# The last layer's attention output on one Trainium2 core: both products turned by matmuls with the identity into one place, without VectorE's sum

## What is computed

```python
scores = jnp.einsum('biph,biqh->biqp', k, q)
tril = jnp.tril(jnp.ones((n, n), dtype=scores.dtype))
triu = jnp.triu(jnp.ones((n, n), dtype=scores.dtype))
masked = scores * tril - NEG_BIG * (1.0 - triu)
attn = jax.nn.softmax(masked / D_HEAD ** 0.5, axis=-1)
z = jnp.einsum('biph,biqp->biqh', v, attn)
z_flat = jnp.transpose(z, (0, 2, 1, 3)).reshape(b, n, -1)
out = jnp.einsum('df,bqf->bqd', W_O, z_flat)
```

## Time and profile before

| | |
|---|---|
| device time, median of 3 runs | 3890.96 us (3883.97 to 3895.62) |
| the profiled execution | 3896.18 us |
| its span | 3893.9 us |
| mean granted TensorE clock | 0.887 of full speed |
| busy: VectorE, TensorE, ScalarE, GpSimd | 88%, 80%, 75%, 34% of the span |

### The profile page before, as it was taken

One profiled execution on the slowest core, in us unless ns is written; L12 is line 12 of the kernel. 1 busy time (PEld: TensorE's weight loads), 2 busy tenths in 40 slices (PEclk: granted clock), 3 DMA queues, 4 the chain that ended last, 5 costly groups with the idle time before them and its releaser, 6 DMA issues.

```text
span 3893.9 us, 31221 instructions
## 1 busy us (share of the span) xinstructions
PE 3127.3 (80%) x8728; PEld 1368.3 (35%) x8728; DVE 3420.1 (88%) x4654; ACT 2925.3 (75%) x3806; POOL 1337.2 (34%) x644
## 2 busy tenths in 40 slices
PE   5655878889787788979888888979788887877797
PEld 3231423334343333424343333424343333432232
DVE  1499979999898999999999999999999998999822
ACT  2546887987868888787888878787888879686442
POOL 0254333333323334343433443343433433333200
PEclk8757788989888899989999999989989999888797
DMA  1233333424324243333434342343424333333310
GB/s 63 77 108 96 113 109 92 128 80 135 99 94 118 93 131 95 119 118 109 125 98 123 107 131 94 121 117 109 124 95 126 104 116 104 104 119 104 100 49 11
DMA packets 209022, 404.60 MB, mean 104 GB/s; under 512 B 25936, under 2 KB 34256, under 8 KB 208592
## 3 DMA queue, kind: packets, MB, share of 16 engines
q1 hardware_dynamic: 206800, 398.41, 32.8%
q0 software_dynamic: 2048, 4.20, 1.0%
HBM read 387.57 MB, written 14.94 MB: 103 GB/s over the span
## 4 chain that ended last, share of the span: by engine, by line
PE 37%; DVE 26%; ACT 25%; issue 12%; POOL 0%; DMA 0%; DVEq 0%; ACTq 0%; POOLq 0%
PE bank_a L569 8%; DVE states L921 7%; PE bank_b L580 7%; ACT L705 6%; DVE states L927 6%; ACT decay L705 6%; DVE y_sum L932 3%; ACT L701 3%; ACT tok L705 3%; ACT last L705 3%; ACT middle L705 3%; PE bank_p L478 1%; PE bank_c L397 1%; PE bank_p L421 1%; PE bank_c L640 1%
## 5 line engine op out<-in xcount | busy, mean ns | idle before, releaser
L1199 POOL TENSOR_TENSOR dbu<-dtu,b_rows 128x1024 f32<-128x1024 f32 x512 | 1243.4, 2431 | 2104.1 <-DVE states L921 1823.6
L921 DVE TENSOR_TENSOR_SCAN states<-decay,dbu 128x512 f32<-128x512 f32 x1024 | 1298.7, 1311 | 38.1 <-ACT decay L705 30.5
L705 ACT ACTIVATE decay<-dt,neg_a 128x508 f32<-128x508 f32 x1024 | 659.4, 707 | 64.6 <-DVE states L921 59.0
L705 ACT ACT_TABLE_LOAD x516 | 662.0, 1283 | 47.5 <-PEq L344 16.6
L569 PE MATMUL bank_a<-middle,experts 128*128 128x512 f32 x1024 | 616.2, 687 | 97.1 <-ACT middle L705 88.9
L705 ACT ACTIVATE middle<-bank_a,columns 128x512 f32<-128x512 f32 x608 | 417.8, 687 | 329.6 <-PE bank_a L569 305.4
L927 DVE TENSOR_TENSOR states<-states,c_rows 128x512 f32<-128x512 f32 x960 | 610.8, 679 | 0.3
L932 DVE TENSOR_TENSOR y_sum<-y_sum,states 128x512 f32<-128x512 f32 x960 | 609.9, 674 | 0.2
L580 PE MATMUL bank_b<-middle,experts 128*128 128x512 f32 x1024 | 572.7, 643 | 21.4 <-ACT middle L705 11.8
L705 ACT ACTIVATE last<-bank_c 128x512 f32<-128x512 f32 (+2 forms) x320 | 201.0, 634 | 198.0 <-PE bank_c L617 52.4
L701 ACT ACT_TABLE_LOAD x232 | 297.7, 1283 | 46.0 <-PE bank_p L469 17.0
(11 more groups left out here) (206 smaller groups left out, 3944.7 us busy)
## 6 DMA issues: line engine op xcount, KB each, us to landing
b_rows<-bc_scratch SPq DMA_DIRECT2D x512, 256.0 KB, 3.4
c_rows<-bc_scratch SPq DMA_DIRECT2D x512, 256.0 KB, 3.3
experts<-ew SPq DMA_DIRECT2D x128, 512.0 KB, 3.5
comb_rows<-comb_scratch SPq DMA_DIRECT2D x128, 256.0 KB, 3.8
h_scratch<-tok SPq DMA_DIRECT2D x16, 256.0 KB, 3.3
x_scratch<-xin SPq DMA_DIRECT2D x16, 256.0 KB, 3.8
xr<-x_scratch SPq DMA_DIRECT2D x16, 256.0 KB, 4.9
h<-h_scratch SPq DMA_DIRECT2D x16, 256.0 KB, 5.3
```

The source lines that it names most:

```text
L705: return nc.scalar.activation(out, in_, func, **more)
L921: tick(nc.vector.tensor_tensor_scan(hs[:, h, ::step], da[:, n % DECAYS, h, ::step], dbu[:, n % AHEAD, h, ::step], 0.0, ALU.mult, ALU.add), ...
L1199: tick(nc.gpsimd.tensor_tensor(dbu[:, n % AHEAD], dtu[:, k % 2], row, ALU.mult), "a_dbu")
```

## The change

The sum on VectorE goes, with the semaphore `a_z`. `zu` becomes two tiles in turn, as `zs` has, and the second of them is `h3`, which the layer doesn't need at that time. TensorE waits for both products and turns each 128x128 block of both by a matmul with the identity; the second adds into the place of the first. The four order strings of TensorE, ScalarE, VectorE and SyncE are written anew from early on. All pieces are still there, but for VectorE's 64 pieces with the sum; TensorE's string keeps its 2836 letters, VectorE's has 2759.

```diff
@@ ORDER (lines from each string, the rest is like it)
-        "PDCPPPPPPPPPPPPCPPPPPPPPPPPPPPPPPPPPPPPPPPPPPPPPPPPDDDPDCPDPDPPDDPDDPPDPPDPPPPPPPPPPPPPPPPPPPPPPPPPP"
+        "PDCPPPPPPPPPPPPCPPPPPPPPPPPPPPPPPPPPPPPPPPPPPPPPPPPDDPDDPCDPDPPPPPDDPPDDPPDPDPPPPPPPPPPPPPPPPPPPPPPP"
...
-    d_sq, d_xn, h3, zu = (fin[:, i] for i in (0, 1, 2, 5))
+    d_sq, d_xn, h3 = (fin[:, i] for i in (0, 1, 2))
+    zu = fin[:, 5], h3
...
                     else:
                         yield
-                        pe.wait_ge(s["a_z"], x + j + 1)
+                        pe.wait_ge(s["a_zu"], 2 * (x + j + 1))
                         for pr in range(4):
-                            last = nc.tensor.transpose(bk[:, blk(pr)], zs[j % 2][:, blk(pr)], w("ident"))
+                            mm(bk[:, blk(pr)], zs[j % 2][:, blk(pr)], w("ident"), start=True, stop=False)
+                            last = mm(bk[:, blk(pr)], zu[j % 2][:, blk(pr)], w("ident"), start=False, stop=True)
                         tick(last, "a_T")
...
                     tick(tt(eight(z), eight(v[:, j]), wide(e1[:, h]), ALU.mult), "a_zu")
                     yield
-                    if x + j:
-                        dve.wait_ge(s["a_z"], x + j)
                     dve.wait_ge(s["a_sv"], x + j + 1)
-                    tick(tt(eight(zu), eight((C, E)[j % 2]), wide(e0[:, h]), ALU.mult), "a_zu")
-                    yield
-                    dve.wait_ge(s["a_zu"], 2 * (x + j + 1))
-                    tick(tt(z, z, zu, ALU.add), "a_z")
+                    tick(tt(eight(zu[j % 2]), eight((C, E)[j % 2]), wide(e0[:, h]), ALU.mult), "a_zu")
```

More of the change, by code:

```diff
@@ new lines @@
+        "CCCPCCCPCCCPCCCCPCCPPCCPPCCPPCCPCCPPCCDCCDCCDDCCPCCDPCCDCPCCCPDCDDDPPCCDPPCCDPPCCPPDDPDPDCPDPCPDDDDD"
+        "DCDCPDDPCPDCPPDPCCCPDDCCPDCCCCPCDCPPDCCPPDDCCDPPDCCPDCCPCCPCCPCCPCCDDPDPCCPPDCCPPCCPDDDDPCCDCCPCCPDD"
+        "DPDCCDCCDDCCCCDCCDCCCCDCCDCCCCCCCCPDDCPCCPCDPPDCPPCCDPPCCDPCCPCDPCDDDPDCPPDCPDDDCDCDDDCCCPCCDPPDDCCD"
+        "PPCCPPCDCPCCPCCDPPDCCDPPDCCPPDCCPDCCPCCPCDCCCPDPDPCCPPDCCPPCCDPPCCDPDCCPDPDDDCCDCCDCCDCCDDCCPCCDCCDC"
+        "CCCCCCCPCCPCDCCPDCDDPPCDPCCPDPPCCPPPDDPCCPCDPCPDCDDCDDPDCDDCPPDPPDDCCCPPDCCPDPCCDPPDDPPCCDPCCPCCDPDC"
@@ new lines @@
+        "CDCCPCCPCCDCCPDCCPCCDPDCCPPDCCPPCCDPPCCPDCCPCCPCCDDDPDDCCCCPCCDCCDCDCPCCDDCCCCDDCCCCPDCCPDPCPCCPPCPP"
+        "DDCPPDDCCDCCDCCPCPCPPDDDCCDDDDDCDDPDCPPDPPDDCCCPPDCCPDCCDCCDCCDPPPDCCPPDCCPPDDCCPDDCCPCCPCCPCCPCCDPC"
+        "CDPPCCDPPCCPPDPDCCDCCPDDPDDPCCCCDCCDCCDCCDDCCDDCCCCDCCDCCCCCCDCCPCPDCCPDDCPPCDPPCCDPPCCPPPDDCCCPCPDP"
+        "CPDCDDDDCDDDCDDCCCPCCDPPCCDPPDPPDDCCPDCCDCCPCCDPPDCCDPPDCCDPCCPCCDPDCCPCCPCCPCCDPDPCCPPCCPDCCPPPCCPD"
+        "DCCPDPDDPCCCCDCCDCCDCCDCCDCCDDCCCPCDPCCDPPPCCPPCDCCDCPPCDDPCCPCCDPCCDPPPDPDDDDDDCDPCDDPPDCPPCDPPDDPC"
@@ new lines @@
+        "DCPDCCPCPDDCCDPPCCDCCPCPDCCCPDDCCPCCPCCPCCPDDPDCCPPCCDPPCCDPPCCPPPDDPCCDCCDCDDCCCDDCCCCDCCDCCDDCCDDC"
+        "CDCCDCCCCCCCCPCCPCCDDPDDPCPPCCPCPPDPDPCPDDCCPCCPCCDCPPCDDDDCDCDDPDCPPDCPPDDCCCPPDCCPDPCCDPPDDPPCCDCC"
+        "PCCPCCDPDDPDCCPCCPCCPCCDDPCCPPDCCPDPCCPPDPDCCPCCPCDCDDPDDCCCCCCCCDCCDDCCDCCDCCDDCCCCDPCCDCCPCCPCCPPC"
+        "DCCPPCDCDDPPCCPDPCCPDPPPPDDDCCCDPCDDPPDCPPCDDPCPDDCPDDDCCCPCCDPPDCCDPDDPCCPPDCCPDPCCPCCDCCPCCPCCDDDP"
+        "CCDCCPCCPPDPCCDPPCCDDPCCPCPDCCCDDDDPCCCCCCCCDCCDDDDCCDDCCCCDCCDCCCCCCPCCPCDDCCPDDCPPCDPPCCDPPCCPPPDD"
@@ new lines @@
+        "CCPCPDCPPDDCDCDDPDCDDCPPDPPDDCCCPPDCCPDCCDCCDCDCPPPDCCPPDCCPPDDCCPDDCCPCCPCCDCCPDPDPCCPPCCDPPCCDPPCC"
+        "PDDCCPDPDDPCCCCCCDCCDDDDCCDDCCCCDCCDCCCCPCCCPCCCDDPDCCPPCDPCCPCPPDPDCPPPCCCCPCCDDCPDCPDDCDDDCDDPDCPP"
+        "DCPPDDCCCPPDCCPDPCCDPPDDPPCCDCCPCCPCCDPDDPDCCPCCPCCPCCDDPCCPPDCCPDPCCPPDPDCCPCCPCDCDDPDDCCCCCCCCDCCD"
+        "DCCDCCDCCDDCCCCDPCCDCCPCCPCCPPCDCCPPCDCDDPPCCPDPCCPDPPPPDDDCCCDPCDDPPDCPPCDDPCPDDCPDDDCCCPCCDPPDCCDP"
+        "DDPCCPPDCCPDPCCPCCDCCPCCPCCDDDPCCDCCPCCPPDPCCDPPCCDDPCCPCPDCCCDDDDPCCCCCCCCDCCDDDDCCDDCCCCDCCDCCCCCC"
@@ new lines @@
+        "PCCPCDDCCPDDCPPCDPPCCDPPCCPPPDDCCPCPDCPPDDCDCDDPDCDDCPPDPPDDCCCPPDCCPDCCDCCDCDCPPPDCCPPDCCPPDDCCPDDC"
+        "CPCCPCCDCCPDPDPCCPPCCDPPCCDPPCCPDDCCPDPDDPCCCCCCDCCDDDDCCDDCCCCDCCDCCCCPCCCPCCCDDPDCCPPCDPCCPCPPDPDC"
+        "PPPCCCCPCCDDCPDCPDDCDDDCDDPDCPPDCPPDDCCCPPDCCPDPCCDPPDDPPCCDCCPCCPCCDPDDPDCCPCCPCCPCCDDPCCPPDCCPDPCC"
+        "PPDPDCCPCCPCDCDDDDCCCCCCDCDCCCDCCDCCDCCDDCCCCDCCDCCCCCCCDCCDDCCDCCDCCDCCCDDCDDCDDDCDDDDCDCDDCCCDCCDC"
+        "CDCCDCDCDCCDCCDCCDCDCCCDCCDCCDCCDDCCCCDCCCCDDDDCCDCCCCCDDCCCDCCDCCCCCCCCCCCCCCCCCCDDDDDDDDDCDCDCDDCC"
@@ L103 @@
+        "CDCCDCCCCDCDCDCCDCCCCDCCCCCCCCCCCCCCCCDDDDDDDDDDDDDDDDDDDDDDD",
         "",
@@ L137 @@
+        "DDDCCCCCCCDCDCDDDDCCDDCCDCCCCCCCCCCDDDDDDDDDDDDDDDDDDDDDDDD",
         "",
@@ L167 @@
+        "AAAACAAAAAAAAPACAPAACADCCCDCAAAAAACAAAAAAAAADAAAAAAAAAAAAAACACACAAAAAACAAAACAAAAAAAACAAAAACAAADACACC"
+        "AACAAACCCCCCDCCCD",
         "",
```

166 lines of the change are left out of this document (68 added, 98 removed).

## The result

The forecast was a gain of 1.6%, 3830 us (3790 to 3890). The changed kernel takes 3902.83 us (median of 10 runs, 3897.86 to 3910.64) beside 3890.36 us for the kernel before in the same comparison (10 runs, 3883.88 to 3900.90): ratio 1.0027, 95% interval 1.0014 to 1.0040. So there is no gain but a small loss, between 5 and 16 us by the interval. The prediction was wrong in sign and by 73 us.

The account below looks back on a forecast made before the run. It took VectorE to bound the middle groups: -43.4 (sum) - 32 (order strings) + 8 (turning) + 7 (end) = -60.4 us, from 3896.18 to 3835.8 us profiled, so a median of 3830 us, range 3790 to 3890.

Parts of the forecast that it names:

- What bounds the kernel now: Middle groups: each 218.46 us group costs about VectorE's work, 211.89 us busy, 97%; TensorE has 33.3 us free, ScalarE 34.6.
- The sum that goes: VectorE, last layer of fourteen groups: removing the additions saves 3.10 us a group, 43.4 us; lower bound 38.0.
- The turning on TensorE: Eight matmuls replace four transposes: 72 us more TensorE work in fourteen groups, of which 8 us show (2 to 27).
- The end: Last two groups: 10.3 us more TensorE work, 2.9 us back from removed sums, +7 us; lower clock 6.3 us more.
- The order strings: ScalarE's table loads fall from 748 to 686; shorter stretches where VectorE starves gain 32 us (0 to 79.5).
- the two early waits: VectorE's waits of 15.21 and 15.20 us before the fifth and sixth groups' scans, forecast to fall below 10 us.
- The strings give nothing: Rival: the new queues' mixed three-group cycle earns nothing, the 32 us are missing, 3862 us; chance 0.17.
- TensorE becomes what the others wait for: Rival, expert loop: all 72 us on the path, 3894 us, or 3952 us with lower clock; chance 0.22.
- clock part: Part of the TensorE rival: clock falls to its lower level, fourteen groups cost 130 us more, 3952 us; chance 0.09.
- the forecast itself: Main case: median of 3830 us, with its own range of 3800 to 3862; chance 0.52.

Follow-up runs that it names:

- e4: Kernel before with VectorE's sum removed, old order strings, four transposes of the first product alone: 3882.57 us, ratio 0.9972.
- e14: Kernel before without VectorE's sum and without the second product, four transposes, old order strings: 3872.50 us, ratio 0.9945.
- e3: Kernel before with each transpose made into two matmuls with the identity, sum and order strings kept: 3934.78 us, ratio 1.0109.
- e1: Changed kernel with the order strings of the kernel before, only the sum's letters taken out: 3923.36 us, ratio 1.0075.
- e9: Changed kernel with its new order strings, but TensorE turns only the first product by four transposes: 3903.38 us, ratio 1.0022.
- e5: Kernel before with the first layers' Gelu in the expert loop's function, 594 table loads instead of 748: 3911.65 us, ratio 1.0039.
- e6: Kernel before without VectorE's sum, four transposes of the first product, first layers' Gelu in the expert loop's function: 3869.03 us, ratio 0.9940.
- e15: Kernel before with one more 128x512 sum on VectorE for each sequence, into a tile not read there: 3932.29 us, ratio 1.0100.
- e11: Kernel before with filler matmuls that change nothing put into TensorE's waits, two waits at `xin` swapped: 3945.36 us, ratio 1.0139.
- e12: Kernel before with the sum moved from VectorE to GpSimd, old order strings, four transposes: 3975.15 us, ratio 1.0213.
- e7: Kernel before with one transpose instead of four for each sequence, sum on VectorE kept: 3916.70 us, ratio 1.0057.

## Why the prediction was wrong

**"What bounds the kernel now": "in the middle each group costs about what VectorE has to do".** This is the step that failed first. The 97% were read right and stood for nothing more than a share: with 3.5 and 4.4 us less of VectorE's work a middle group still took 218.5 us (e4, e14). Three engines with 212, 185 and 184 us of work in 218 us feed each other through in-order queues, and TensorE's 33 us and ScalarE's 35 us free are nearly all waits for each other and for VectorE. Taking work from VectorE gave it longer waits elsewhere (L1106, +22.5 us in e4). The chain went to ScalarE in e4; in e14 it has TensorE at 38% and the two others at 25% each.

**"The sum that goes", -43.4 (lower bound 38.0).** The work was right: 50.8 us fewer for all sixteen groups. Its worth was 12 us in the old strings, outside the bounds. The clause that it rested on was named, "this needs VectorE to stay the bound", but had no price.

**"The turning on TensorE", +8 (2 to 27).** The work was right: 1.95 to 2.15 us a sequence. It showed at +40 us in the old strings, half of the 82 us of records, above the upper bound taken from the chain's share. A share of the chain is no bound for what an addition costs: e3's chain has TensorE at 42% instead of 37%. The Trainium skill (Perfetto Trace Analysis, Transposes) asks for the transpose in place of a standard matmul; e3 agrees in kind, 40 us for 256 transposes replaced, though by two matmuls each.

**"The end", +7.** Measured from e1 against before, -1.0 us: the turns cost 2.4 (e3), the sum gave 6.7 (e4), not 2.9. That the sum's own waits are on the path of the last groups is argued. The end window of the earlier trace rows, from which the 78% were read, begins at 3448.19, which is no start of L1158; the nearest are 3355.80 and 3591.28.

**"The order strings", -32 (0 to 79.5).** The count of loads, 686, was right, and the two early waits did shrink, from 30.4 to 17.3 us, with the third group's from 23.3 to 7.9. But that was not time won: with the same short waits e9 is 2.7 us later at the fourth cut than e4. And the price of 0.96 us for each us above 23.8 came from four stretches of one trace in which other things changed too. e5 took away 198 us of ScalarE's work and lost 16 us. Against the same instructions the strings are worth -20.5 with long turns and +21 with short ones: their value is how well they fit this very set of durations, and it can't be read off one engine's counts.

**Rivals.** The strings give nothing (0.17) was right in its mark, groups that differ by 13 us; its 3862 us still held the 43 us of the sum, which weren't there. TensorE becomes what the others wait for (0.22) was nearest: 3894 us, no change. It was held down to 0.22 by "33.3 us free in a group", the same reading of a share as a reserve. Its clock part came in small: the granted clock fell from 0.94 to 0.90 in the middle, not to the lower level throughout. The bounds named for the range of the forecast itself add up to 3877 us at the upper end, not 3862; the measured time lies above both.

**What stays open.** The middle groups in the old strings keep to three lengths that lie equally far apart: about 218.4 us (before, e4, e5, e6, e14), 222 us (e1, e3, e15) and 225.3 us, here one of e11's, five of which follow each other:

```profile
2066.50:2291.78 225.28, 194.00 (x564) 83.95 (x563) 211.95 (x290) 184.10 (x240) 83.57 (x41) 0.95 0.36 111
```

e12 has 225.3 us too, with 217.1 us of VectorE's work. Groups between these lengths occur (219.9 us in before, 223.8 in e3, and e7's lie from 220.6 to 223.2), but don't repeat. The granted clock keeps step with a group of such a length: in before's groups that begin at 1603.66, 1822.07 and 2040.54 it falls to the lower level at the same distances from the group's start, to a tenth of a microsecond (0.50 in 2 us from 1618.40, 1836.90 and 2055.40). This is a rival to the account by queues alone: a small addition may cost a whole jump to the next length (e15, 2.4 us more on VectorE), and a small relief nothing. It isn't the whole either, since e14's relief of 4.4 us is more than the distance between two lengths and brought no shorter group. Whether the clock holds the length or the length the clock's pattern isn't shown. How much of the new strings' 26 us in the middle is the lower clock, and how much the order of the instructions, no run separates: each kernel that changed the clock changed the work too. I had no kernel that holds the order and sets the clock.

## What to carry over

A busy share of 97% isn't a reserve of 3% elsewhere: in a planned set of in-order queues measure each engine's margin in both directions, one more and one less of a cheap instruction, before pricing an exchange between engines (here 23 to 54 us for 34 us more on VectorE, and 12 us back for 51 us less). An edit that comes with a new order is two changes; run the old order with the new code and the reverse, since the same edit was worth -12 in one and -68 in the other. And price TensorE's work together with its granted clock: a shorter matmul sequence can make the rest slower.

## What the runs showed of the hardware

- A turn by eight float32 matmuls with the identity, two for each 128x128 block, is 1.95 to 2.15 us for 128x512; four transposes are 0.66 us.
- Leaving out 192 transposes lowered the mean granted clock from 0.887 to 0.880, and 1024 unchanged matmuls took 626.7 us instead of 616.2.
- A 128x512 float32 sum takes 1436 ns on GpSimd (e12) and 780 on VectorE. VectorE's `dtu` takes 2.84 us beside GpSimd's `dbu` and 0.75 us without it (17 and 47 of e12's 64).
- Settled middle groups take 218.4, 222 or 225.3 us, and the granted clock falls at the same places in each of them (before, e11).
- Behind a table load of 1283 ns the activation started at once: in the earlier trace rows the load that began at 1020.47 ended at 1021.75, and the Gelu began at 1021.76.
